# First attention on one Trainium2 core: row update ahead of the first guess, constants and centring behind the differences, squares behind the exponential, output bias on GpSimd

## What is computed

```python
q = _ln((x @ Wq + bq).reshape(b, s1, H, HD), qn_w, qn_b)          # _layernorm(x) comes in as x
kv = ... y_main @ Wk + bk, y_main @ Wv + bv                        # last 16 context rows: Wkv_dca, bkv_dca
k = _ln(kv[..., :HD], kn_w, kn_b);  v = kv[..., HD:]
ctx = _attn(qT, k, v) + DCA_WEIGHT * _attn(qT, k_dca, v_dca)       # 16 heads of 16, softmax over 48 and over 16 keys
return ctx @ Wo + bo                                               # added to the un-normalised x
```

## Time and profile before

| | |
|---|---|
| time, median of 3 runs | 745.77 us (744.7 to 746.88) |
| the profiled execution | 745.7 us, its span 743.9 us |
| first attention in it | about 20 to 183 us |
| busy in the span: PE, DVE, ACT, POOL | 91%, 74%, 65%, 58% |
| mean granted TensorE clock | 0.972 of full speed |

### The profile page before, as it was taken

The page is one execution under the profiler, slowest core; times in us unless marked ns, Lnnn a source line. Parts: engine busy times, 40 slices in busy tenths (PEclk is TensorE's granted clock), DMA queues, the critical chain, the costliest instruction groups (busy, mean ns, idle before and its releaser), DMA issues. The chain is left out here.

```text
span 743.9 us, 16268 instructions
## 1 busy us (share of the span) xinstructions
PE 679.7 (91%) x5814; PEld 540.2 (73%) x5814; DVE 549.4 (74%) x1180; ACT 481.2 (65%) x982; POOL 431.9 (58%) x635
## 2 busy tenths in 40 slices
PE   2789999987999989999999999999999999978794
PEld 1567667665888877888888888888888888765452
DVE  3699999986487877767676676676766766746886
ACT  1377777763566577666666666666666666647993
POOL 2487787774677734656666656666666655435500
PEclk9799999997999999999999999999999999999996
DMA  9200001300311000000000000000000000000001
GB/s 285 59 9 12 10 9 46 134 2 19 110 58 30 7 15 2 15 22 16 16 30 8 22 23 22 22 15 17 29 8 23 9 1 2 1 1 1 30 29 57
DMA packets 26019, 22.83 MB, mean 31 GB/s; under 512 B 5041, under 2 KB 24402, under 8 KB 25810
## 3 DMA queue, kind: packets, MB, share of 16 engines
q1 hardware_dynamic: 24160, 20.92, 9.0%
q10 hardware_dynamic: 1778, 0.86, 0.4%
HBM read 19.67 MB, written 2.10 MB: 29 GB/s over the span
## 5 line engine op out<-in xcount | busy, mean ns | idle before, releaser
L678 POOL TENSOR_TENSOR rstd<-var,minus_half 128x8 f32<-128x8 f32 x65 | 107.7, 1657 | 5.1
L654 POOL TENSOR_TENSOR pr<-pr,rstd 128x256 f32<-128x256 f32 x64 | 39.2, 613 | 80.2 <-DVE pr L950 80.2
L669 POOL TENSOR_TENSOR p_n<-pr,pinv 128x256 f32<-128x256 f32 x64 | 39.3, 614 | 79.3 <-DVE pinv L911 79.3
L1565 PE MATMUL banks<-m_hi,z_hi 128*128 128x256 f32 x256 | 75.0, 293 | 7.5 <-DVE z_lo L903 7.4
L1189 ACT ACTIVATE kT<-banks,gk_q 128x512 f32<-128x512 f32 x64 | 44.0, 688 | 52.1 <-PE banks L1574 52.1
L1565 PE MATMUL banks<-m_hi,z_lo 128*128 128x256 f32 x256 | 72.5, 283 | 0.0
L1565 PE MATMUL banks<-m_lo,z_hi 128*128 128x256 f32 x256 | 72.4, 283 | 0.0
L903 DVE TENSOR_TENSOR z_lo<-banks,z_hi 128x512 fp32r<-128x512 f32 x64 | 43.9, 686 | 31.0 <-ACT z_hi L1155 31.0
L946 DVE TENSOR_REDUCE pmax<-banks 128x4 f32<-128x256 f32 x64 | 27.0, 422 | 48.2 <-PE banks L1610 48.2
L930 DVE TENSOR_REDUCE sums<-q_sq 128x4 f32<-128x512 f32 x64 | 43.7, 683 | 25.2 <-ACT q_sq L1170 25.2
L1565 PEld LDWEIGHTS banks<-m_hi,z_hi 128*128 128x128 f32 x256 | 48.6, 190 | 17.5 <-DVE z_lo L903 15.9
(11 more groups left out here) (191 smaller groups left out, 2101.5 us busy)
## 6 DMA issues: line engine op xcount, KB each, us to landing
w_raw<-in_L_xattn_Wq SPq DMA_DIRECT2D x4, 512.0 KB, 5.8
wo_raw<-in_L_xattn_Wo SPq DMA_DIRECT2D x1, 2048.0 KB, 8.2
k_ctx<-in_ctx SPq DMA_DIRECT2D x16, 128.0 KB, 2.7
w_raw<-in_L_ffn_w_gating SPq DMA_DIRECT2D x16, 128.0 KB, 2.4
out_x<-x_sb SPq DMA_DIRECT2D x4, 512.0 KB, 2.9
x_sb<-in_x SPq DMA_DIRECT2D x1, 1536.0 KB, 9.5
a_ctx<-in_ctx SPq DMA_DIRECT2D x16, 64.0 KB, 1.8
w_raw<-in_L_xattn_Wk SPq DMA_DIRECT2D x2, 512.0 KB, 9.0
```

The lines of the kernel that those rows point to most:

```text
L654: pool.tensor_tensor(pr[:, 1 - par, :, :], pr[:, 1 - par, :, :], rstd1[:, par, HC:2 * HC].unsqueeze(2).to_broadcast([P, HC, S]), ALU.mult) ...
L669: pool.tensor_tensor(p_n[:, 1 - par, :, :], pr[:, 1 - par, :, :], pinv[:, 1 - par, :].unsqueeze(2).to_broadcast([P, HC, S]), ALU.mult).the ...
L678: pool.tensor_tensor(rstd1[:, par, :], var1[:, :], minus_half[:, :].to_broadcast([P, 2 * HC]), ALU.pow).then_inc(root1, 1)
L1565: last = nc.tensor.matmul(bank[6][:, za * D:(za + 1) * D], z[:, odd, c, :], mm[:, h, :], start=w % NS == 0 and c == 0 and m == 0, stop=w % ...
```

## The change

On VectorE the row update of tile i-2 moves up between the square sum and the first guess of tile i+1; the constants of the weight rounding move from ahead of the maxima to behind centring, so that centring directly follows the differences. On ScalarE the squares of tile i+2 move up from behind the queries' copy to directly behind the exponential. The output bias no longer goes through TensorE: its two matmuls go, and GpSimd adds it to the row of x_sb with one instruction of 128x256 behind its roundings, for tile i-1 in step i. The row update waits for that as well. `b_room` takes the place of `ones_row`, with the same size.

```diff
--- before.py
+++ after.py
@@ -223,7 +223,7 @@
         qk_half = sb(sa, "qk_half", [P, 2, 2 * H])
         bvT = sb(sa, "bvT", [P, KD, P])
         prm = sb(sa, "prm", [P, D])
-        ones_row = sb(sa, "ones_row", [P, P])
+        b_room = sb(sa, "b_room", [P, 128])
 
 
         a_cT = sb(sa, "a_cT", [P, 2, 2, PER, S])
@@ -321,7 +321,7 @@
         exp_ready, inv_ready, prob_ready = sem("exp_ready"), sem("inv_ready"), sem("prob_ready")
         pt_done, pt_evac = sem("pt_done"), sem("pt_evac")
         o_done, o_evac, y_done = sem("o_done"), sem("o_evac"), sem("y_done")
-        ones_set, x_updated = sem("ones_set"), sem("x_updated")
+        x_biased, x_updated = sem("x_biased"), sem("x_updated")
         stored = sem("stored")
         cent_ready, sum_ready, max_ready, shifted = sem("cent_ready"), sem("sum_ready"), sem("max_ready"), sem("shifted")
         row_steps = sem("row_steps")
@@ -586,7 +586,6 @@
                                base=0, pattern=[[-1, P]], channel_multiplier=1).then_inc(consts, 1)
             pool.memset(a_cT[:], 0.0).then_inc(zeros, 1)
             pool.memset(v_blk[:], 0.0).then_inc(zeros, 1)
-            pool.memset(ones_row[0:1, :], 1.0).then_inc(ones_set, 1)
             pool.memset(v_blk2[:], 0.0).then_inc(zeros, 1)
             pool.memset(qk_sq[:, :, HD0:HD0 + 1], 0.5 * QK_EPS).then_inc(eps_set, 1)
             roots(pool, 0, 0)
@@ -613,6 +612,13 @@
                     pool.tensor_tensor(w0_raw[:, part], w0_raw[:, part], rnd2[:, c % 2, :, 0], ALU.add).then_inc(w0_steps, 1)
                     pool.wait_ge(w0_steps, 2 * c + 1)
                     pool.tensor_tensor(w0[:, part], w0_raw[:, part], rnd2[:, c % 2, :, 0], ALU.subtract).then_inc(w0_steps, 1)
+                t = i - 1
+                if live(t, NT):
+
+                    if t == 0:
+                        pool.wait_ge(bo_ready, 1)
+                    pool.wait_ge(xhat_ready, t + 1)
+                    pool.tensor_tensor(x_sb[:, t, :], x_sb[:, t, :], bo_bc[:, :], ALU.add).then_inc(x_biased, 1)
                 t = i
                 if live(t, NT):
 
@@ -751,14 +757,19 @@
                     dve.wait_ge(sq_ready, t + 1)
                     after(dve, scaled, t - 1)
                     dve.tensor_reduce(half2[:, t % 2, :, 0], qk_sq[:, :, :], AX.X, ALU.add).then_inc(ln_steps, 1)
+                t = i - 2
+                if live(t, NT):
+
+                    dve.wait_ge(y_done, t + 1)
+                    dve.wait_ge(x_biased, t + 1)
+                    dve.tensor_tensor(x_sb[:, t, :], y_bank(t)[:, 0:D], x_sb[:, t, :], ALU.add).then_inc(x_updated, 1)
+                    dve.wait_ge(x_updated, t + 1)
+                    dve.bn_stats(row_bn[:, t, :], x_sb[:, t, :]).then_inc(row_steps, 1)
+                    moments(dve, 1, t, 1)
+                t = i + 1
+                if live(t, NT):
                     dve.wait_ge(ln_steps, LN_N * t + 1)
                     first_guess(dve, LN_N * t + 1, half2[:, t % 2, :, 0], rstd2[:, t % 2, :, 0], qk_tmp[:, t % 2, :])
-                for c in chunks(i):
-
-                    if c == 0:
-                        dve.wait_ge(w0_in, 3 * 16)
-                    after(dve, w0_steps, 2 * (c - 1))
-                    e4m3_magic(dve, magic_steps, 2 * c, w0_raw[:, c * W_CHUNK:(c + 1) * W_CHUNK], rnd2[:, c % 2, :, 0])
                 t = i
                 both = banks[:, 5 * 512:7 * 512].rearrange("p (h s) -> p h s", s=S)
                 if live(t, NT):
@@ -772,14 +783,6 @@
                     for seg, (lo, hi) in enumerate(((0, MAIN), (MAIN, S))):
                         dve.tensor_tensor(prob[:, t % 2, :, lo:hi], both[:, :, lo:hi],
                                           smax[:, seg, :].unsqueeze(2).to_broadcast([P, H, hi - lo]), ALU.subtract).then_inc(shifted, 1)
-                t = i - 2
-                if live(t, NT):
-
-                    dve.wait_ge(y_done, t + 1)
-                    dve.tensor_tensor(x_sb[:, t, :], y_bank(t)[:, 0:D], x_sb[:, t, :], ALU.add).then_inc(x_updated, 1)
-                    dve.wait_ge(x_updated, t + 1)
-                    dve.bn_stats(row_bn[:, t, :], x_sb[:, t, :]).then_inc(row_steps, 1)
-                    moments(dve, 1, t, 1)
                 t = i + 2
                 if live(t, NT):
 
@@ -788,6 +791,12 @@
                     after(dve, sq_ready, t - 1)
                     dve.tensor_tensor(qk_cent[:, t % 2, :, :].rearrange("p h d -> p (h d)"), bank[1][:, :],
                                       bqk[:, :, :].rearrange("p s n -> p (s n)"), ALU.add).then_inc(cent_ready, 1)
+                for c in chunks(i):
+
+                    if c == 0:
+                        dve.wait_ge(w0_in, 3 * 16)
+                    after(dve, w0_steps, 2 * (c - 1))
+                    e4m3_magic(dve, magic_steps, 2 * c, w0_raw[:, c * W_CHUNK:(c + 1) * W_CHUNK], rnd2[:, c % 2, :, 0])
                 if i == 0:
                     dve.wait_ge(bo_done, 1)
                     dve.wait_ge(bo_in, 16)
@@ -1075,6 +1084,11 @@
                 if live(t, NT):
                     act.wait_ge(shifted, 2 * (t + 1))
                     act.activation(prob[:, t % 2, :, :], prob[:, t % 2, :, :], ACT.Exp, scale=SCALE0).then_inc(exp_ready, 1)
+                t = i + 2
+                if live(t, NT):
+                    act.wait_ge(cent_ready, t + 1)
+                    after(act, ln_steps, LN_N * (t - 1) + 1)
+                    act.activation(qk_sq[:, :, 0:HD0], qk_cent[:, t % 2, :, :], ACT.Square, scale=SQ_SCALE).then_inc(sq_ready, 1)
                 t = i - 1
                 if live(t, NT):
                     act.wait_ge(o_done, t + 1)
@@ -1090,11 +1104,6 @@
                     after(act, s_group, GRP * t)
                     act.activation(qT0[:, :, :].rearrange("p c n -> p (c n)"), bank[3][:, 0:D], ACT.Identity,
                                    scale=cols[:, 0, 0:1], bias=cols[:, 0, 1:2]).then_inc(t_evac, 1)
-                t = i + 2
-                if live(t, NT):
-                    act.wait_ge(cent_ready, t + 1)
-                    after(act, ln_steps, LN_N * (t - 1) + 1)
-                    act.activation(qk_sq[:, :, 0:HD0], qk_cent[:, t % 2, :, :], ACT.Square, scale=SQ_SCALE).then_inc(sq_ready, 1)
                 t = i + 1
                 if live(t, NT):
                     turned_keys(t, 0)
@@ -1367,14 +1376,10 @@
                 t = i - 1
                 if live(t, NT):
 
-                    if t == 0:
-                        pe.wait_ge(bo_ready, 1)
-                        pe.wait_ge(ones_set, 1)
+                    pe.wait_ge(o_evac, t + 1)
                     after(pe, x_updated, t)
-                    nc.tensor.matmul(y_bank(t)[:, 0:D], ones_row[0:1, :], bo_bc[0:1, :], start=True, stop=False)
-                    pe.wait_ge(o_evac, t + 1)
                     for kk in range(KD):
-                        last = nc.tensor.matmul(y_bank(t)[:, 0:D], oT[:, kk, :], wo0[:, kk, :], start=False, stop=kk == KD - 1)
+                        last = nc.tensor.matmul(y_bank(t)[:, 0:D], oT[:, kk, :], wo0[:, kk, :], start=kk == 0, stop=kk == KD - 1)
                     last.then_inc(y_done, 1)
                 t = i + 1
                 if live(t, NT):
```

## The result

| | before | after |
|---|---|---|
| time, median of 7 runs each | 746.23 us (744.7 to 747.78) | 741.47 us (740.46 to 743.99) |
| ratio after to before | | 0.9941, 95% interval 0.9924 to 0.9958 |
| the profiled execution | 745.7 us, span 743.9 | 742.46 us, span 740.7 |

The change made the kernel faster by 0.6%; the forecast was no change (746.0 us). The profiled executions lie 3.2 us apart, the medians 4.8: the profiled one of after is one of its slower runs.

What follows compares the result with a forecast made beforehand. VectorE was taken to set the first attention's period, with some instructions held by GpSimd. Start +1.0, middle +1.1 and end -1.8 gave +0.3 us on 745.7: 746.0 us, with 741.2 to 749.4 for 8 in 10.

Steps and rivals of the forecast that it cites:

- Holds of the constants: VectorE's L429 and L431, moved behind centring, stand still through long GpSimd instructions; the move costs some 0.85 us.
- N: Start of GpSimd's refinement of a tile (L402), from which the prediction counts its times in us.
- The period: One tile's cycle in the first attention, set by VectorE: 8.99 us against 8.89 before.
- L412 is held to N+8.24: The guess's first step on VectorE, due at N+7.71, meets the second half of GpSimd's scaling of the probabilities.
- the change doesn't free the guess: Rival, chance 0.13: L412 and L414 both held as before, next refinement at N+8.79, time 743.8 us.
- middle: Eleven periods from tile 3 to tile 14 at 8.99 us instead of 8.89: +1.1 us.
- Start: Start of the stage, where GpSimd has no slack: its bias addition costs +1.0 us by tile 3, at most +1.6.
- End: End of the stage: bias matmuls gone, tile 14's row update without constants ahead: -1.8 us, bounds 0 and -2.9.
- later stages are unchanged and start behind it: Stages after the first attention add nothing of their own to the stage's +0.3 us.
- Faster rival: L429 passes beside GpSimd's normalisation and only L431 waits: period 8.61, time 741.5 us, chance 0.19.
- The signs: Trace marks named beforehand: L412 about 0.5 us, L414 0.19, tile 3 about 1 later, FFN's first matmul within 1 of 182.96.

Runs made afterwards that it cites:

- v1: Kernel before with the new order (row update, constants, squares) from step 15 on and GpSimd's bias for tiles 14 and 15 only: 743.48 us, ratio 0.9963.
- w1: Kernel before with only the row update moved, from step 15 on: 744.67 us, ratio to before 0.9983.
- x1: Kernel before with useless TensorE matmuls added in steps 14, 15 and 16: 747.20 us, ratio to before 1.0003.
- v3: Changed kernel with the constants ahead of the maxima up to step 14, behind centring in steps 15 and 16: 736.41 us, ratio to before 0.9867.
- v2: Changed kernel with the old order from step 15 on and the bias of tiles 14 and 15 on TensorE: 746.92 us, ratio to before 1.0005.
- w2: Kernel before with only the output bias changed, added by GpSimd for all tiles: 745.28 us, ratio to before 0.9999.
- w3: Kernel before with only the row update moved, in all steps: 740.39 us, ratio to before 0.9928.
- u1: Changed kernel with the constants ahead of the maxima again in all steps: 738.72 us, ratio to before 0.9907.
- u2: Changed kernel with the output bias as two matmuls on TensorE again: 744.90 us, ratio to before 0.9965.

## Why the prediction was wrong

- **Holds of the constants: right.** L429 0.88 and L431 0.71 where "about 0.7" each was expected; sums start at N+4.50 where N+4.42 stood. The rule of the Trainium skill ("SBUF — State Buffer", section "Who interferes with whom"), that tensor_scalar on SBUF operands can stand still until a GpSimd instruction that came first has ended, agrees with the trace at L429, which no row of before could show: 0.88 us, ending 0.15 after L606.
- **The period: direction off by a small amount.** 8.87 measured, 8.99 predicted, 8.89 before. The step that failed is "L412 is held to N+8.24". L412 came at N+7.65 instead of N+7.71, and the first half of L621 (now L627) ended at N+7.70 instead of N+7.63 (it starts at N+6.23, and this half takes 1.47 us by the trace of before). So L412 slipped in between the halves, and only L414 was held (0.49). The next N came 0.58 us behind the end of L627, which is the rule of the rival "the change doesn't free the guess" (8.79, here 8.86 since L627 starts 0.07 later). In the middle that rival, given 0.13, was the right one. The period at 8.87 held in the middle; the two steps with row roots took 9.20 and 9.17 (8.89 and 8.90 before), a term of 0.6 us which the sum had left at nothing. From tile 3 to tile 14 that makes 98.17 us against 97.76: +0.4, not +1.1.
- **Start: mis-sized.** From the maxima of tile 0 to those of tile 3 it is 28.62 us before and 29.07 after: +0.45 where +1.0 stood. The maxima of tile 0 came 0.9 us earlier in this execution. Traces of the old order at that place (before, v1, w1, x1) had them between 31.3 and 32.0, and 26.98 to 28.92 us from there to tile 3, so all of this may be scatter; it isn't settled.
- **End: right in sum, not in its parts.** From the maxima of tile 14 to the FFN's first matmul: 24.74 before, 23.02 after, -1.7 for a forecast of -1.8. But the last maxima, freed of their wait for GpSimd's rounding, met another, of 2.08 us, for TensorE's scores, and didn't come earlier (168.09). TensorE was granted 0.50 from 160 to 164 us, where before had 0.82, which may be why (argued only); in v3, with the same order there, they came 8.32 us behind those of tile 14 instead of 9.93. The -1.7 came wholly behind the last maxima.
- **The step that failed most: "later stages are unchanged and start behind it".** It put TensorE's clock at the FFN's start at nothing. The same 23 matmuls took 6.57 us before and 4.95 after. This term of 1.6 us is the largest that the sum lacks, though the lower clock could be read before: the earlier trace rows has the first of them at 0.88 us, and the trace of before a granted clock of 0.74 in that stretch.
- **Faster rival: right in its time by luck.** 741.5 us was named for constants that aren't both held. They were; the time came from elsewhere. Its 0.19, and the 0.26 for faster in all, were too small because every gain was taken from one walk with the clock held fixed.
- **The signs.** L412 was to take 0.5 and L414 0.19: they took 0.15 and 0.49. GpSimd's wait ahead of the scaling was 0.30 (0.2 named). Tile 3 came 0.47 us earlier, not 1 later, tile 14 level, not 2 later, and the FFN's first matmul lay 1.78 us from 182.96, not within 1.

In account: tile 0 -0.9, start +0.45, middle +0.4, end -1.7, FFN's start -1.6, together -3.4; the spans differ by 3.2. These are two executions, and part of the account is where the clock happened to be low in them, as v1's trace shows. The medians differ by 4.8. How much of that is clock is an estimate: each run's mean granted clock has its median at 0.972 over the 93 runs of before beside the experiments and 0.979 over 7 of after, and over those 93 runs the time falls by 0.3 us for each us less at the lower level. 0.007 of 743 us, twice counted because the lower level is half (0.50 in the rows), is 10 us less at the lower level, so some 3 us of the 4.8. The mean clocks of the two profiled executions differ by 0.002 only (0.972 and 0.974), some 1 us of their 3.2 by the same estimate: what after gained at the FFN's start it partly lost before it. x1 shows that TensorE's waits in the last steps move its clock. Why the whole change moves it more than v1 (0.974), v2 (0.972), w1 (0.975), w2 (0.976) or w3 (0.977) stays open, and with it how the gain divides between order and clock.

## What to carry to other kernels

When an instruction is moved on VectorE, look at what GpSimd runs at the new place: the same two constants cost 0.6 us beside short GpSimd instructions (0.29 and 0.30) and 1.6 beside long ones (0.88 and 0.71), and the change gave back in every period what another part of it had won. Undoing one part of a change that is faster as a whole (u1, then v3) found 5 us more than the change itself (736.41 against 741.47; 1.7 us of it may be clock in stages that weren't changed). And where a stage ends in waits of TensorE, the first matmuls of the next stage belong in the sum at the clock that they will be granted.

## What the runs showed of the hardware

- A held VectorE instruction goes on at the boundary between two GpSimd instructions that follow back to back; where an instruction of 128x32 arrives just there it isn't held at all (L412, 0.15 us, started 0.05 ahead of the boundary). One of 128x256 ends 0.15 us behind the boundary (L429 and L431 of after).
- Time and TensorE's mean granted clock go together in the runs of one program: u2's ten runs, one program, lie between 739.18 us at a mean of 0.985 and 749.25 us at 0.965.
- Filling TensorE's waits with useless matmuls raised the clock (0.971 to 0.980, and 0.981 to 0.988) and gained no time in either kernel.
